# Selective scan: C rows by broadcast DMA from DRAM, the input products of 5 of 16 states on GpSimd, three rotating PSUM slots

## What is computed

```python
def step(h, inp):
    u_t, d_t, B_t, C_t = inp
    dA = jnp.exp(d_t[..., None] * As)
    h = h * dA + (d_t * u_t)[..., None] * B_t[:, :, None, :]
    y = jnp.einsum('bkcn,bkn->bkc', h, C_t)
    return (h, y)
...
x_dbl = jnp.einsum('bkdl,kcd->bkcl', xs, x_proj_w)
dts, Bs, Cs = jnp.split(x_dbl, [R, R + N], axis=2)
dts = jax.nn.softplus(dts + dt_projs_b[None, :, :, None])
As = -jnp.exp(A_logs).reshape(K, DI, N)
out_y = selective_scan(xs, dts, As, Bs, Cs, Ds.reshape(K, DI))
```

## Time and profile before

| What | us |
|---|---|
| median of 3 runs | 2875.15 |
| range of the runs | 2874.18 to 2876.72 |
| span of the profiled execution (first to last instruction) | 2873.3 |
| DVE busy in it | 1730.5 (60%) |
| POOL busy | 1130.2 (39%) |
| ACT busy | 1209.8 (42%) |
| PE busy | 2285.8 (80%) |

### The profile page before, as it was taken

The page is one execution under the profiler, slowest core; times in us unless marked ns, Lnnn a source line. Parts: engine busy times, 40 slices in busy tenths (PEclk is TensorE's granted clock), DMA queues, the critical chain, the costliest instruction groups (busy, mean ns, idle before and its releaser), DMA issues.

```text
span 2873.3 us, 21891 instructions
## 1 busy us (share of the span) xinstructions
PE 2285.8 (80%) x6404; PEld 1036.0 (36%) x6404; DVE 1730.5 (60%) x1473; ACT 1209.8 (42%) x1316; POOL 1130.2 (39%) x517
## 2 busy tenths in 40 slices
PE   4797777877777787777877777899886499999991
PEld 2342322333333333332333323445554244444440
DVE  2437999999999999999999995621222000000002
ACT  1226666666666576666666642111111122222220
POOL 0003777667676666767667760000001300000004
PEclk9898999999999999999999997799997699999996
DMA  5201000000000000000000004100001422222205
GB/s 187 66 22 33 1 0 0 0 0 0 0 0 0 0 0 0 0 0 0 0 0 0 0 9 165 44 1 1 0 0 40 177 88 88 88 88 88 88 11 186
DMA packets 42372, 105.57 MB, mean 37 GB/s; under 512 B 4559, under 2 KB 30259, under 8 KB 41058
## 3 DMA queue, kind: packets, MB, share of 16 engines
q1 hardware_dynamic: 38242, 93.53, 9.2%
q0 software_dynamic: 4096, 11.62, 1.3%
HBM read 74.64 MB, written 28.31 MB: 36 GB/s over the span
## 4 chain that ended last, share of the span: by engine, by line
PE 45%; issue 23%; DVE 17%; ACT 8%; POOL 4%; DMA 1%; DVEq 1%; ACTq 0%; SPq 0%; POOLq 0%
PE ps L937 9%; PE ps L949 9%; DVE ps L1076 8%; PE ps L720 4%; ACT arena L504 3%; POOL arena L379 3%; DVE arena L1084 3%; PE ps L664 2%; PE ps L903 2%; PE ps L701 2%; PE ps L789 2%; PE ps L828 2%; PE ps L675 2%; PE ps L691 2%; ACT arena L512 1%
## 5 line engine op out<-in xcount | busy, mean ns | idle before, releaser
L379 POOL TENSOR_TENSOR arena<-arena 128x1024 f32<-128x1024 f32 x384 | 976.0, 2542 | 437.7 <-DVE arena L1084 422.9
L1084 DVE TENSOR_TENSOR_SCAN arena<-arena,ps 128x1024 f32<-128x1024 f32 x384 | 877.9, 2286 | 13.3
L720 PE MATMUL ps<-arena 128*128 128x512 f32 x1536 | 777.9, 631 | 43.0 <-DVE arena L1063 40.1
L701 PE MATMUL ps<-arena 96*128 (+1 forms) x1536 | 424.3, 395 | 274.9 <-DVE arena L1084 235.9
L512 ACT ACTIVATE arena<-ps 128x1024 f32<-128x1024 f32 x384 | 392.4, 1022 | 437.6 <-PE ps L701 436.8
L1076 DVE TENSOR_TENSOR ps<-ps,arena 128x1024 f32<-128x1024 f32 x384 | 465.9, 1213 | 35.1 <-PE ps L701 32.6
L504 ACT ACTIVATE arena<-arena 128x1024 f32<-128x1024 f32 x384 | 438.6, 1142 | 0.3
L720 PEld LDWEIGHTS ps<-arena 128*128 128x128 f32 x1536 | 309.5, 202 | 313.1 <-issue 251.4
L701 PEld LDWEIGHTS ps<-arena 96*128 96x128 bf16 x1536 | 126.5, 100 | 689.0 <-DVE arena L1084 446.7
L1291 DVE TENSOR_TENSOR arena<-ps,arena 128x384 f32<-128x384 f32 x32 | 17.8, 558 | 579.2 <-PE ps L949 579.2
L937 PE MATMUL ps<-arena 128*128 128x512 f32 x576 | 258.3, 610 | 20.2 <-ACT arena L616 20.2
(11 more groups left out here) (161 smaller groups left out, 1688.2 us busy)
## 6 DMA issues: line engine op xcount, KB each, us to landing
arena<-in_w SPq DMA_DIRECT2D x16, 2304.0 KB, 14.3
arena<-in_xT SPq DMA_DIRECT2D x4, 1536.0 KB, 9.3
slot_in<-arena SPq DMA_DIRECT2D x8, 768.0 KB, 15.9
arena<-in_x_tok SPq DMA_DIRECT2D x1, 6144.0 KB, 20.4
arena<-slot_in SPq DMA_DIRECT2D x8, 768.0 KB, 16.1
slot_out<-arena SPq DMA_DIRECT2D x8, 768.0 KB, 4.6
out<-arena SPq DMA_DIRECT2D x8, 768.0 KB
z_scratch<-arena SPq DMA_DIRECT2D x4, 768.0 KB, 5.5
```

What stands on the lines that cost most here:

```text
L379: nc.gpsimd.tensor_tensor(hst[:, u % RING], hst[:, u % RING], c_sb[:, u % RING], ALU.mult).then_inc(p2_ok, 1)
L701: mm = pe.matmul(dst[:, h * 512:(h + 1) * 512], sel_lhs[0:BR, n], bc[0:BR, q // J, dr, m, h * 512:(h + 1) * 512], start=True, stop=True)
L720: mm = pe.matmul(Y_PS[:, h * 512:(h + 1) * 512], ident, hst[:, u % RING, h * 512:(h + 1) * 512], start=(u == 0), stop=(u == UN - 1))
L1084: nc.vector.tensor_tensor_scan(h, f, x, 0.0, ALU.mult, ALU.add).then_inc(sc_ok, 1)
```

## The change

The arrangement of the scan stage is changed in four places; the arithmetic per element stays.

- In the x_proj steps ACT also copies the B and C rows, unsplit, to rows, and SP stores them to DRAM (bc_dram, L340 of the changed kernel). Only B is still split and placed in bc, with three DMAs a step in place of six.
- C rows are no longer spread by PE and copied by ACT. SP loads each from DRAM into c_sb, broadcast over the partitions by two DMAs, one per image and half of the partitions (row_to, L344 of the changed kernel). c_sb is a ring of four: a C row waits for the read-out four units back.
- For the states in ON_POOL (2, 5, 8, 11, 14) the B row comes the same way, into the unit's own buffer of hst, now a ring of eight, and POOL multiplies it by dux in place (make_input), four units ahead of the read-out beside it (LEAD). The row is issued two units ahead of the C row beside it (AHEAD), and waits for the addition to Y_PS eight units back. PE doesn't spread that B row and DVE doesn't multiply; DVE scans from hst into hst.
- Three PSUM slots (SLOT3) rotate over 17 events per direction: the 16 units and the delta product, which had C_PS. A unit of DVE's uses its slot for the B row; a unit of POOL's for its decay, written there by ACT. The other decays have a ring of three. LAG is 4.

```diff
-RING = 4
-LAG = 3
+ON_POOL = (2, 5, 8, 11, 14)
+NSLOT = 3
+HRING = 8
+CRING = 4
+LEAD = 4
+LAG = 4
+AHEAD = 2
...
+def pool_units(u):
+    return u // N * len(ON_POOL) + sum(n in ON_POOL for n in range(u % N))
+def ring_uses(units, slot, ring, before):
+    return sum(u % ring == slot for u in units if u < before)
+POOL_UNITS = [u for u in range(UN) if u % N in ON_POOL]
+FED = {slot: ring_uses(POOL_UNITS, slot, HRING, UN) for slot in range(HRING)}
+VEC = N - len(ON_POOL)
+DELTA = "delta"
+def event(n):
+    return n + (n > DT_AT)
+def slot_holder(e):
+    e -= NSLOT
+    if e < 0:
+        e = max(k for k in range(N + 1) if k % NSLOT == (e + NSLOT) % NSLOT) - (N + 1)
+        return e
+    if e == DT_AT + 1:
+        return DELTA
+    return e - (e > DT_AT)
+def decay_slot(n):
+    return sum(k not in ON_POOL for k in range(n)) % NSLOT
+def decay_holder(n):
+    vec = [k for k in range(-N, N) if k % N not in ON_POOL]
+    return max(k for k in vec if k < n and decay_slot(k % N) == decay_slot(n))
...
-        B_PS = [pair_of_banks(0), pair_of_banks(2)]
-        C_PS, Y_PS = pair_of_banks(4), pair_of_banks(6)
+        Y_PS = pair_of_banks(6)
+        def slot_of(n):
+            return SLOT3[event(n) % NSLOT]
+        DT_PS = SLOT3[(DT_AT + 1) % NSLOT]
...
-                        for m in range(2):
-                            sp.dma_start(bc[part * SR:part * SR + SR, p * 2 + o, dr, m, :],
-                                         parts[H2 + m * SR:H2 + m * SR + SR, k % 2, part]).then_inc(bc_st[k % 2], 16)
+                        sp.dma_start(bc[part * SR:part * SR + SR, p * 2 + o, dr, :],
+                                     parts[H2:H2 + SR, k % 2, part]).then_inc(bc_st[k % 2], 16)
+                    sp.wait_ge(rows_ok, p * K + (k + 1))
+                    sp.dma_start(bc_dram[p * 2 + o, dr].rearrange("m r s -> (m r) s"), rows[H2:P, k % 2]).then_inc(rows_st[k % 2], 16)
+            def row_to(dst, q, dr, m, n, done):
+                for im in range(2):
+                    sp.dma_start(dst[H2 * im:H2 * im + H2], bc_dram[q // J, dr, m, im * N + n, :].partition_broadcast(H2)).then_inc(done, 16)
+            def b_row(q, u, first):
+                dr, n = divmod(u, N)
+                if not (first and u < HRING):
+                    sp.wait_ge(ya_ok, q * UN + (u + 1))
+                row_to(hst[:, u % HRING], q, dr, 0, n, b_ld[u % HRING])
+            def c_row(q, u, first):
+                dr, n = divmod(u, N)
+                if not (first and u < CRING):
+                    sp.wait_ge(p2_ok, q * UN + (u + 1))
+                row_to(c_sb[:, u % CRING], q, dr, 1, n, c_ld[u % CRING])
+            def feed(q, first, last):
+                for u in range(UN):
+                    if u + AHEAD < UN:
+                        if u + AHEAD in POOL_UNITS:
+                            b_row(q, u + AHEAD, first)
+                    elif not last and u + AHEAD - UN in POOL_UNITS:
+                        b_row(q + 1, u + AHEAD - UN, False)
+                    c_row(q, u, first)
+            sp.wait_ge(split_ok, 4 + 2 * K * NP)
+            sp.wait_ge(dts_ok, 2 + K * NP)
+            for k in range(2):
+                sp.wait_ge(z_st[k], 1 + 16 * NP)
+                sp.wait_ge(bc_st[k], 1 + K * NP // 2 * PLACED)
+                sp.wait_ge(rows_st[k], 1 + K * NP // 2 * 16)
+            for u in range(AHEAD):
+                if u in POOL_UNITS:
+                    b_row(0, u, True)
+            feed(0, True, False)
+            with nc.sync.Fori(1, NQ - 1) as q:
+                feed(q, False, False)
+            feed(NQ - 1, False, True)
...
+            def make_input(q, u):
+                dr, slot = u // N, u % HRING
+                pool.wait_ge(du_ok, q * 2 + (dr + 1))
+                pool.wait_ge(b_ld[slot], q * (32 * FED[slot]) + 32 * (ring_uses(POOL_UNITS, slot, HRING, u) + 1))
+                nc.gpsimd.tensor_tensor(hst[:, slot], hst[:, slot], dux[:, dr], ALU.mult).then_inc(in_ok, 1)
             def read_outs(q, last):
                 for u in range(UN):
                     dr, n = divmod(u, N)
                     U = q * UN + u
+                    if u + LEAD < UN:
+                        if u + LEAD in POOL_UNITS:
+                            make_input(q, u + LEAD)
+                    elif not last and u + LEAD - UN in POOL_UNITS:
+                        make_input(q + 1, u + LEAD - UN)
                     pool.wait_ge(sc_ok, U + 3)
-                    pool.wait_ge(c_free, U + 2)
-                    nc.gpsimd.tensor_tensor(hst[:, u % RING], hst[:, u % RING], c_sb[:, u % RING], ALU.mult).then_inc(p2_ok, 1)
+                    pool.wait_ge(c_ld[u % CRING], q * (32 * UN // CRING) + 32 * (u // CRING + 1))
+                    nc.gpsimd.tensor_tensor(hst[:, u % HRING], hst[:, u % HRING], c_sb[:, u % CRING], ALU.mult).then_inc(p2_ok, 1)
...
+                    act.wait_ge(rows_st[k % 2], p * (K * 16 // 2) + (1 + k // 2 * 16))
+                    nc.scalar.activation(rows[H2:P, k % 2], SLOT3[k % 2][H2:P], ACT.Copy).then_inc(rows_ok, 1)
+                    nc.scalar.activation(parts[H2:H2 + SR, k % 2, 0], SLOT3[k % 2][H2:H2 + SR], ACT.Copy).then_inc(hi_ok, 1)
                     nc.scalar.activation(dts[0:DR, p * 2 + o, dr, :], SLOT3[k % 2][0:DR], ACT.Copy).then_inc(dts_ok, 1)
                     act.wait_ge(split_ok, p * (2 * K) + (4 + 2 * k + 1))
-                    nc.scalar.activation(parts[H2:P, k % 2, 1], rest[H2:P, k % 2], ACT.Copy).then_inc(mid_ok, 1)
+                    nc.scalar.activation(parts[H2:H2 + SR, k % 2, 1], rest[H2:H2 + SR, k % 2], ACT.Copy).then_inc(mid_ok, 1)
...
-                    if not (first and u < RING):
-                        act.wait_ge(sc_ok, U + (3 - RING))
-                        settled(act)
-                    nc.scalar.activation(decay[:, u % RING], dlt[:, dr], ACT.Exp,
-                                         scale=a_neg[:, q % OJ, dr, n:n + 1]).then_inc(dec_ok, 1)
+                    if n in ON_POOL:
+                        held, dst = slot_holder(event(n)), slot_of(n)
+                    else:
+                        held, dst = decay_holder(n), decay[:, decay_slot(n)]
+                    if held == DELTA and last and dr:
+                        held = slot_holder(DT_AT + 1)
+                    if held == DELTA:
+                        act.wait_ge(dtev_ok, q * 2 + (dr + 2))
+                    elif not (first and dr * N + held < 0):
+                        act.wait_ge(sc_ok, q * UN + (dr * N + held + 3))
+                    settled(act)
+                    nc.scalar.activation(dst, dlt[:, dr], ACT.Exp, scale=a_neg[:, q % OJ, dr, n:n + 1]).then_inc(dec_ok, 1)
                     if n == ACT_AT[0] and not (last and dr):
                         delta_parts(q + dr, 1 - dr, 0)
-                    act.wait_ge(c_ok, U + 1)
-                    act.wait_ge(p2_ok, U + 1)
-                    nc.scalar.activation(c_sb[:, u % RING], C_PS, ACT.Copy).then_inc(c_free, 1)
...
+            def slot_free(q, dr, e, first, last):
+                held = slot_holder(e)
+                if held == DELTA and last and dr:
+                    held = slot_holder(DT_AT + 1)
+                if held == DELTA:
+                    pe.wait_ge(dtev_ok, q * 2 + (dr + 2))
+                elif not (first and dr * N + held < 0):
+                    pe.wait_ge(sc_ok, q * UN + (dr * N + held + 3))
             def tile_steps(q, first, last):
                 for u in range(UN):
                     dr, n = divmod(u, N)
-                    U = q * UN + u
-                    pe.wait_ge(sc_ok, U + 1)
-                    spread(q, u, 0, B_PS[u % 2]).then_inc(b_ok, 1)
-                    after_dt = n == DT_AT + 1 and not (last and dr)
-                    if after_dt:
-                        add_trailing_y(q, u, first)
-                        pe.wait_ge(dtev_ok, q * 2 + (dr + 2))
-                    pe.wait_ge(c_free, U + 1)
-                    spread(q, u, 1, C_PS).then_inc(c_ok, 1)
-                    if not after_dt:
-                        add_trailing_y(q, u, first)
+                    if n not in ON_POOL:
+                        slot_free(q, dr, event(n), first, last)
+                        spread(q, u)
+                    add_trailing_y(q, u, first)
                     if n == DT_AT and not (last and dr):
-                        pe.wait_ge(c_free, U + 2)
+                        slot_free(q, dr, DT_AT + 1, first, last)
                         delta_product(q + dr, 1 - dr)
...
-                    dve.wait_ge(b_ok, U + 1)
-                    nc.vector.tensor_tensor(B_PS[u % 2], B_PS[u % 2], dux[:, dr], ALU.mult).then_inc(p1_ok, 1)
-                    dve.wait_ge(p1_ok, U + 1)
-                    dve.wait_ge(dec_ok, U + 1)
-                    dve.wait_ge(ya_ok, U + 1)
-                    h, f, x = hst[:, u % RING], decay[:, u % RING], B_PS[u % 2]
+                    h = hst[:, u % HRING]
+                    if n in ON_POOL:
```

(11 more changed lines are left out.)

53 lines of the change are left out of this document (30 added, 23 removed).

## The result

The changed kernel takes 3010.74 us (3009.29 to 3012.52, 4 runs) where the kernel before takes 2874.66 us (2873.23 to 2876.72, 4 runs) on the same chip: ratio 1.0468, 95% interval [1.0453, 1.0482]. The forecast was 2909 us with a range of 2745 to 2970. The sign was right; the size is outside the range by 41 us.

A forecast was written before the change was run, and what follows sets the result against it. VectorE bounds the scan stage before; after, POOL with its waits for row loads, 62.3 us a direction against 61.2. Span 2873.3 + 26 (stage) + 6 (x_proj) + 2 (fill, drain) = 2907, median 2909 us, range 2745 to 2970.

The forecast's parts named there:

- L = 6.9 us: POOL's loop through DMA: from a read-out's end to the B row's landing, four DMAs 5.3 us, plus 1.5 fixed, 0.1 wake.
- upper bound of 7.5: L in us with the fixed cost of a load from DRAM, w_out, 2.1 us in place of 1.5.
- The step to unit 2 is POOL's own.: POOL, into the next direction: six multiplies, 14.2 us, just over the load loop's 14.0, so no wait for the row.
- Both loops: Step to unit 2: POOL's six multiplies, 14.2 us, and the loop through read-out 11, 3 x 2.36 + 6.9 = 14.0.
- Rival 2: Row loads cost more than the z row: at L = 7.5, 2967 us; dearer than 7.5 or the clock, together 0.08.
- z row: Store of z from 64 partitions, 786,432 bytes in 5.5 us; gave the loads 197 GB/s and 1.5 us fixed cost.
- The fit from the same page: About 2.0 us plus bytes over 436 GB/s per DMA: would make L 4.4 us and let POOL run without a gap.
- rival 3: TensorE at 1.2 GHz all the time needs some 74 us a direction, is the bound: 3190 us; with dearer loads, 0.08.
- Rival 1: POOL-bound, faster: load halves overlap, L at or under 5.1 us, 55.3 us a direction, stage 1327, 2741 us; chance 0.11.
- 53.5 us on VectorE: VectorE per direction after losing 5 of 16 products: 59.13 - 5 x 1.25 = 52.9 us, with half an evacuation 53.5.
- fill and drain: Ends of the longer chain (product, row load, LAG 4): adds 2 us.
- Would-show list: Profile signs: POOL idle before L468, DVE idle, L344's landing times and rate, POOL busy near 1413 us, tile pitch.

The follow-up runs named there:

- f2: The changed kernel with SP's loop over the tiles written out, nothing else: 2965.62 us, ratio 1.0302 to the kernel before.
- f3: The changed kernel with one row load into all 128 partitions in place of two into halves (image 2 gets image 1's rows): 2855.43 us, ratio 0.9928.
- g2: The changed kernel with each row load bringing 512 of 1024 columns from the second tile on, same number of DMAs: 2865.83 us, ratio 0.9970.
- h3: As h1, but each row load brings 512 of 1024 columns from the second tile on: 2818.49 us, ratio 0.9797 to the kernel before.
- h1: The changed kernel with AHEAD 3 in place of 2, SP's tile loop written out and LAG 3 in place of 4: 2824.05 us, ratio 0.9816.
- j3: h1 with VectorE waiting for its own product last before the scan, and the first delta step on ScalarE: 2796.91 us, ratio 0.9714.
- f1: The changed kernel with B rows asked for one unit earlier (AHEAD 3 in place of 2): 2857.58 us, ratio 0.9927 to the kernel before.
- j2: h1 with the first delta step on ScalarE in place of VectorE: 2798.96 us, ratio 0.9727 to the kernel before.

## Why the prediction was wrong

**What the change costs in engine work.** Right for POOL: a multiply takes 2.35 us (forecast 2.36), queued ones follow without a gap, and the page has 1378 us busy (forecast 1413; the read-outs are stretched less than before, 945.6 us against 976.0). In the stage POOL takes (1597.1 - 316)/24 = 53.4 us a direction without its waits; the forecast had 62.3 - 4 x 2.2 = 53.5. The scan with the decay in PSUM costs what the other costs, 2272 against 2287 ns. ACT and TensorE gained nothing, as put.

**The loop through DMA.** The mechanism was right: POOL stands before L468 for DMA, later read-outs queue behind, nothing refills it. Two terms of it failed.

- *L = 6.9 us.* From read-out to product it measured 7.5 us (mean of the 95 plain cycles): 0.2 for SP to wake, 3.64 for the first load, 3 x 1.20 for the others, 0.1 from the last landing to the product. The fixed part was too small: 1.5 us, where 3.64 - 1.2 = 2.4 are measured. The transfer was too large: 1.33 us from the store's 197 GB/s, where 1.2 are measured (1.13, 232 GB/s, over the whole stage). The eight waits a tile are 22.4 us, not 8 x 2.2 = 17.6: 4.8 x 12 = 58 us of the stage. My upper bound of 7.5 met the value by luck: its fixed part of 2.1 was still too small, and the transfer that was too large made up for it.
- *"The step to unit 2 is POOL's own."* It is not: unit 2 waits 3.31 and unit 18 0.63 us, 3.9 x 12 = 47 us. Both loops were level in my sum (14.2 against 14.0), so with L = 7.5 they wait some 0.4 us, and any delay of SP shows in full. SP's queue has a branch there, 4.4 us without an instruction, and the forecast put it at nothing without looking at it. In f2, without the branch, unit 2 waits 0.59 us: 2.7 x 12 = 33 of the 47 us are the branch, the rest is L.

58 + 47 = 105 us; the stage is 1597.1 - 1495 = 102 us over the forecast. Rival 2 put L at 7.5 and got 2967, inside the range; with the branch's 42 us (f2's difference) that is 3009. So L took the time to the end of the range, and the branch took it out. Rival 2's number was luck too, since its reason, rows dearer than the z row, holds for the fixed part only. That halves of a row don't overlap is shown by the landings, and by f3 and g2 together. The Trainium skill, "DMA: Bandwidth & Descriptors", "Rules for kernel authors", says so too. The fit from the same page was wrongly used in the prediction: its section is on DMAs that GpSimd issues and gives the fit per DMA, and I put four DMAs of SP's in as one of 1 MB. The 4.4 us that came of it are refuted by the 7.5 us here; the fit as the page gives it no run here tests.

**TensorE's clock** (rival 3) is not the cause: the granted clock was 0.84 over the span and 0.80 in the stage (0.95 before), but of SP's waits before L344 only 1.0 us is released by the y additions, and POOL waits for DMA alone. (At half the clock its sum is 2 x 38.2 = 76.4 us, not 74, which changes nothing here.)

**Rival 1, 2741 us,** is out of reach for another reason than L. With the rows in time (h3) the stage is 58.7 us a direction, not 55.3, and VectorE sets it, not POOL. The step "53.5 us on VectorE" was too small by 3.6 us of delta steps and 1.3 us of gaps (53.5 + 4.9 = 58.4). I had read the turn-taking on POOL's side only, where the earlier trace rows show it, because before the change POOL's read-out always came behind VectorE's step, by 0.16 us in all 92 steps of the stage. With products in the queue POOL is already running when the step comes, and VectorE is the one that waits. The Trainium skill, "SBUF — State Buffer", "Who interferes with whom", states that issue order decides who blocks, and that a VectorE operation with two SBUF inputs contends with a POOL operation that reads SBUF. The traces agree for L1156, L1161 and L1166, which have two; L1152 has one SBUF input, so that sentence doesn't cover it, and it was held up all the same. The traces also show more: in 11 of 23 cases the loser stood through the POOL operation under way and one (L1152 in h1) or two (L1156 in j3) more, and POOL then had nothing ready. In the other 12 it got in behind the operation under way (once behind the one after that), and POOL's next operation had begun without a gap. What decides between the two no run shows.

**Outside the stage** +6.3 us, 5.3 of them ahead of it (256.7 against 251.4), forecast 6 and 2 for fill and drain: right.

**Would-show list.** Forecast 2.2 us a wait, 210 us in all, tile 124 to 125; measured 2.5 to 3.0, 316 us in 119 waits, tile 133.6. VectorE idle near 200: 226. About 180 GB/s: 165. Landing in 3 to 7 us: 3.4 to 9.4, median 5.0.

## What to carry to other kernels

When work is moved behind a DMA, write the loop down: which end frees the slot, how many transfers stand in the queue before the one that is waited for, and what the consumer can do meanwhile. Here one more unit of look-ahead was worth 153 us. Look also at what is in the issuing queue besides the transfers (its loop branch, a slot that a later stage frees). And where two engines take turns, a price read while one of them waited for the other says nothing of the price when its queue is full.

## What the runs showed of the hardware that I had not expected

- SP's loop branch at a tile's end: 4.1 to 4.6 us from the branch to the next instruction in the nine times that it goes back, 0.05 us the tenth time. With the loop written out the stage is 41.8 us shorter.
- VectorE operations of 0.67 and 1.20 us that took up to 6.0 us (one L1152 in f1) and 7.6 us (one L1156 in j2) beside a POOL with a full queue. Beside POOL's plain multiplies, product and scan (an operand in PSUM) kept their 1.21 and 2.29 us.
- A register operation and a semaphore wait between product and scan on VectorE went with a gap of 0.19 us in place of 0.04, 210 times a run; with the product waited for last it was 0.13, in all 264. Why 0.09 us of it stay is open.
